# Keys and values of five batches made ahead, and three projections of the second attention in rounded parts

## Time and profile before

| | |
|---|---|
| median of 3 executions | 1377.33 us (1376.74 to 1379.98) |
| the profiled execution's own time | 1384.91 us |
| its span, first to last instruction | 1383.1 us |
| mean granted TensorE clock | 0.975 of 2.4 GHz |
| PE busy | 1311.7 us, 95% |
| DVE, ACT, POOL busy | 65%, 57%, 43% |
| attention(0), to about | 356 us |
| moe0, from about | 363 us to 804 us |
| attention(1), to about | 1191 us |

### The profile page before, as it was taken

One profiled execution on the slowest core, in us unless ns is written; L12 is line 12 of the kernel. 1 busy time (PEld: TensorE's weight loads), 2 busy tenths in 40 slices (PEclk: granted clock), 3 DMA queues, 4 the chain that ended last, 5 costly groups with the idle time before them and its releaser, 6 DMA issues.

```text
span 1383.1 us, 37361 instructions
## 1 busy us (share of the span) xinstructions
PE 1311.7 (95%) x14572; PEld 1155.6 (84%) x14572; DVE 901.4 (65%) x2468; ACT 793.5 (57%) x1750; POOL 596.3 (43%) x522
## 2 busy tenths in 40 slices
PE   6999999998799999999999979999999999899898
PEld 5888888886699999999999968888998998655476
DVE  4788888886576555555655026888888886412287
ACT  3666666564377777777776425556555665332354
POOL 1244444343287777877776033433333431100131
PEclk9999999999699999999999978999999999999999
DMA  5574545461467777777776711731111110399912
GB/s 194 196 246 147 175 144 179 142 224 50 170 209 229 229 226 220 222 222 223 225 224 223 308 54 33 240 136 47 48 48 48 48 40 17 134 415 430 370 56 70
DMA packets 103614, 237.19 MB, mean 171 GB/s; under 512 B 8976, under 2 KB 85904, under 8 KB 91024
## 3 DMA queue, kind: packets, MB, share of 16 engines
q1 hardware_dynamic: 97296, 218.02, 45.7%
q0 software_dynamic: 6144, 16.79, 4.0%
HBM read 173.96 MB, written 60.82 MB: 170 GB/s over the span
## 4 chain that ended last, share of the span: by engine, by line
PE 86%; DVE 6%; DMA 3%; issue 2%; ACT 2%; POOL 1%; SPq 0%; DVEq 0%; ACTq 0%; PEldq 0%; POOLq 0%
PE ps L1337 13%; PE psT L1322 7%; PE psS L520 5%; PE ps L686 5%; PE ps L641 5%; PE psT L529 4%; PE ps L546 4%; PE ps L653 4%; PE ps L552 4%; PE psS L1322 3%; PE ps L1322 3%; PE ps L577 3%; PE ps L626 2%; PE ps L660 2%; PE psT L535 2%
## 5 line engine op out<-in xcount | busy, mean ns | idle before, releaser
L1290 POOL TENSOR_TENSOR wb_lo<-arena,wb_hi 128x2048 fp32r<-128x2048 f32 x64 | 296.4, 4632 | 97.8 <-ACT wb_hi L1409 97.8
L1337 PE MATMUL ps<-wb_hi,hT_hi 128*128 128x256 f32 x528 | 152.4, 289 | 0.8 <-DVE hT_lo L1463 0.8
L529 PE MATMUL psT<-arena 32*128 32x128 f32 x2048 | 152.4, 287 | 0.0
L1006 POOL TENSOR_TENSOR arena<-arena,eps_sb 128x1 f32<-128x1 f32 x96 | 23.9, 249 | 291.7 <-DVE arena L878 198.9
L1337 PE MATMUL ps<-wb_lo,hT_hi 128*128 128x256 f32 x528 | 147.7, 280 | 0.0
L1337 PE MATMUL ps<-wb_hi,hT_lo 128*128 128x256 f32 x528 | 147.6, 280 | 0.0
L520 PE MATMUL psS<-arena 32*128 32x256 f32 x1024 | 143.3, 399 | 0.7 <-ACT arena L798 0.7
L1409 ACT CAST wb_hi<-arena 128x1024 fp32r<-128x1024 f32 x128 | 130.5, 1045 | 8.1 <-DMA arena<-w_dram 7.6
L529 PEld LDWEIGHTS psT<-arena 32*128 32x128 f32 x2048 | 127.7, 190 | 1.1 <-issue 1.1
L920 DVE TENSOR_REDUCE arena<-psS 128x8 f32<-128x1024 f32 x64 | 78.4, 1225 | 49.6 <-PE psS L520 49.6
L520 PEld LDWEIGHTS psS<-arena 32*128 32x128 f32 x1024 | 95.4, 192 | 13.4 <-issue 11.3
(11 more groups left out here) (325 smaller groups left out, 3704.8 us busy)
## 6 DMA issues: line engine op xcount, KB each, us to landing
arena<-wset_dram SPq DMA_DIRECT2D x24, 2048.0 KB, 14.5
xs_rows<-arena SPq DMA_DIRECT2D x33, 1024.0 KB, 8.3
arena<-w_dram SPq DMA_DIRECT2D x32, 1028.0 KB, 6.1
arena<-w_dram SPq DMA_DIRECT2D x32, 1024.0 KB, 5.9
arena<-w_dram SPq DMA_DIRECT2D x7, 2052.0 KB, 12.3
w_sb<-xs_rows SPq DMA_DIRECT2D x33, 256.0 KB, 2.7
xs_rows<-arena SPq DMA_DIRECT2D x33, 256.0 KB, 5.5
arena<-ctxT_dram SPq DMA_DIRECT2D x63, 128.0 KB, 2.3
```

The costliest lines, as they stand in the source:

```text
L529: nc.tensor.matmul(psT[:, b, j * P:(j + 1) * P], kbd[p, (k - 1) % 3, c, par, :], qT[p, (k - 1) % 3, c, :], start=j == 0, stop=False, skip_ ...
L1290: nc.gpsimd.tensor_tensor(wb_lo[:, u % 2, part], wb_raw[:, u % 2, part], wb_hi[:, u % 2, part], ALU.subtract).then_inc(w_g.sem, 1)
L1337: last = nc.tensor.matmul(ps[5][:, t * D:(t + 1) * D], hp[:, f, t * P:(t + 1) * P], wp[:, f, :], start=f == 0 and t == 0 and n == 0, stop= ...
```

## The change

**Five batches ahead.** Keys and values of batches 3 to 7 of attention(1) are made in the last steps of attention(0). SP issues five loads of ctx (128 KB each) at step B-1, into ctxT, xh and xT, after the last queries. PE makes keys 0 of the five in step B+2 after 577's place, its values after 609's place, the second batch after the product at 696, the third to fifth after 708. ACT copies each PSUM bank of 128x512 to SBUF (`put_away`), the first two in the steps, the others at the start of routing. PE waits for all five copies before `turned(0)`. In attention(1), the steps for these batches have no keys and values on PE; ACT reads kbd and vz from the stash. Their ctx loads of 128 KB leave attention(1).

**Rounded parts.** A helper `thrice` makes three float32r products in place of one f32 product. It is used for the values of the batches from 8 on (24 of them), the output projection of all 32 batches, and the dv projection of all 32. ACT makes the rounded weights (three copies of 128x512 after the early batches), POOL the rests (three subtractions in steps 0 to 2). For each batch from 8 on, POOL makes ctx_hi and ctx_lo (128x256 each) one step ahead; for each batch, POOL makes x1_hi and x1_lo (128x256 each) after 769; ACT writes aT in rounded form, and DVE makes aT_lo (128x256 from PSUM) ahead of the maxima at 920. Both POOL pairs stand ahead of 1046 in POOL's stream.

**Moves.** The slots' table is loaded at step B+2, after the last output projection, and no longer at step 9. In unit 0 of moe0 the first weight roundings for unit 1 stand after gelu 1 and gelu 2.

```diff
+                    if A and k == B - 1:
+                        sp.wait_ge(kv_p.sem, kv_p.at(B - 1, "V"))
+                        sp.wait_ge(pre_p.sem, pre_p.at(B - 1, "Q"))
+                        for n_ in range(STASH):
+                            sp.dma_start(stash_ctx[n_]..., a["ctxT"][3 + n_]).then_inc(ld_stash[n_], 16)
...
-                    if not A and k == 5 + EARLY_SETS:
+                    if not A and k == B + 2:
+                        sp.wait_ge(o_p.sem, o_p.at(B - 1, "O"))
                         sp.dma_start(dead[:, 0:12 * P], a["slots"]).then_inc(ld_slots, 16)
...
+                def thrice(out_, left, right):
+                    for n_, (i_, j_) in enumerate(((0, 0), (0, 1), (1, 0))):
+                        for c in range(C):
+                            last = nc.tensor.matmul(out_, left[i_][:, c, :], right[j_][:, c, :],
+                                                    start=n_ == 0 and c == 0, stop=n_ == 2 and c == C - 1)
...
                 def values(i, bank):
+                    if not A and i >= early:
+                        pe.wait_ge(ctx_g.sem, ctx_g.at(i, "lo"))
+                        return thrice(ps[bank][:, D:2 * D], (ctx_hi, ctx_lo), split["v1"]).then_inc(kv_p.sem, 1)
...
+                def ahead_keys(n):
+                    if n == 0:
+                        pe.wait_ge(ld_w, 16)
+                        pe.wait_ge(ex_a.sem, ex_a.at(B - 1, "b"))
+                    pe.wait_ge(ld_stash[n], 16)
+                    ...
...
-                    if valid(k + 1) and k + 1 >= early:
+                    if valid(k + 1) and k + 1 >= early and not stashed(k + 1):
...
+                            pe.wait_ge(aT_v.sem, aT_v.at(k - 2, "lo"))
+                            last = thrice(ps[7][:, D:2 * D], (aT_hi, aT_lo), split["o1"])
...
+                        pe.wait_ge(x1_g.sem, x1_g.at(k - 4, "lo"))
+                        thrice(ps[5][:, D:2 * D], (x1_hi, x1_lo), split["dv"]).then_inc(x1_p.sem, 1)
...
                         last.then_inc(prep_p, 1)
+                        ahead_keys(1)
+                        ahead_values(1)
...
+                        for n_ in range(2, STASH):
+                            ahead_keys(n_)
+                            ahead_values(n_)
...
+                def put_away(n):
+                    act.wait_ge(stash_p, n + 1)
+                    nc.scalar.copy(stash[n], ps[stash_bank[n]][:, :]).then_inc(stash_a, 1)
...
+                    if not A and valid(out_i):
+                        dve.wait_ge(av_a.sem, av_a.at(out_i, "aT"))
+                        before(dve, o_p.sem, o_p.at(out_i - 1, "O"))
+                        nc.vector.tensor_tensor(aT_lo[:, :, :], ps[7][:, 0:D]..., aT_hi[:, :, :], ALU.subtract)
...
+                    if not A and valid(k - 4):
+                        pool.wait_ge(x1_a.sem, x1_a.at(k - 4, "xT"))
+                        before(pool, x1_p.sem, x1_p.at(k - 5, "V"))
+                        nc.gpsimd.tensor_scalar(x1_hi[:, :, :], v, 1.0, 0.0, ALU.mult, ALU.add).then_inc(x1_g.sem, 1)
+                        pool.wait_ge(x1_g.sem, x1_g.at(k - 4, "hi"))
+                        nc.gpsimd.tensor_tensor(x1_lo[:, :, :], v, x1_hi[:, :, :], ALU.subtract).then_inc(x1_g.sem, 1)
+                    if not A and valid(k + 2) and k + 2 >= early + STASH:
+                        ...ctx_hi, ctx_lo in the same way, after the load of batch k+2
...
+                pe.wait_ge(stash_a, STASH)
                 turned(0)
...
-                    if u == 0:
-                        rounded_half(1, 0, 0)
-                        rounded_half(1, 0, 1)
+                        if u == 0 and b in (1, 2):
+                            rounded_half(1, 0, b - 1)
```

More of the change, by code:

```diff
@@ L29 @@
 EARLY_SETS = 4
+STASH = 5
 EARLY_PAIRS = 6
@@ L142, in build @@
         att = carve(H, DH)
+        aT_at = place[0]
         aT = carve(C, P)
@@ L151, in build @@
         mrest = carve(G, 4)
+        spare_at = place[0]
         xn = carve(3, D)
@@ L228, in build @@
         place[0] = max(place[0], attention_used)
+        stash_near = carve(4, 2 * D)
         yb = carve(2, 2, D)
         zero = carve(D)
-        xoff = carve(C, 2 * P)
-        assert place[0] <= attention_end, place[0]
+        assert stash_near is not None and place[0] <= attention_end, place[0]
         place[0] = max(attention_used, 12224)
@@ L451, in attention, with stashed, kv @@
             early_bank = (6, 7, 3)
+            if not A:
+                ctx_g = track(n + "ctx_g", "hi lo", B, base=-2 * (early + STASH))
+            def stashed(i):
+                return not A and early <= i < early + STASH
+            def kv(i):
+                return i if A or i < early else i - STASH
             def ctx_of(i):
@@ L728, in values, with stashed_keys, stashed_values @@
                         .then_inc(kv_a.sem, 1)
+                def stashed_keys(i):
+                    for par in range(2):
+                        last = nc.scalar.activation(kbd[:, i % 3, :, par, :],
+                                                    stash[i - early][:, 0:D].rearrange("p (c t) -> p c t", c=C), ACT.Identity,
+                                                    bias=0.0, scale=cv["parity"][:, par:par + 1])
+                    last.then_inc(kv_a.sem, 1)
+                def stashed_values(i):
+                    nc.scalar.copy(vz[:, i % 3, :, 0, :], stash[i - early][:, D:2 * D].rearrange("p (h d) -> p h d", h=H))\
+                        .then_inc(kv_a.sem, 1)
+                def put_away(n):
+                    act.wait_ge(stash_p, n + 1)
+                    nc.scalar.copy(stash[n], ps[stash_bank[n]][:, :]).then_inc(stash_a, 1)
                 if A:
@@ L741, in scalar @@
                         values(i, early_bank[i])
+                    for name in ("o1", "v1", "dv"):
+                        nc.scalar.copy(split[name][0][:, :, :], w[name]).then_inc(hi_a.sem, 1)
                 for k in steps:
@@ L1124, in scalar @@
             def scalar(act):
+                for n in range(2, STASH):
+                    act.wait_ge(stash_p, n + 1)
+                    nc.scalar.copy(stash[n], ps[stash_bank[n]][:, :]).then_inc(stash_a, 1)
                 act.wait_ge(route_v.sem, route_v.at(0, "ex"))
```

109 lines of the change are left out of this document (88 added, 21 removed).

## The result

The changed kernel takes 1368.95 us in the median of seven executions (1366.81 to 1373.01), the kernel before 1378.74 beside it (1376.74 to 1380.67). The ratio is 0.9933, 95% interval 0.9919 to 0.9947: 9.8 us faster where 17.6 were forecast. The time lies inside the range given, 1353 to 1372, and away from the forecast of 1359.7.

A forecast was written before the change was run, and what follows sets the result against it. PE was taken to bound attention(1), with engines and transfers taking turns at the border to moe0. Rounding 13.6, five batches 4.0 and border 0 sum to 17.6 us, from 1377.33 to 1359.7 us, range 1353 to 1372.

The forecast's parts named there:

- Rounding, 13.6 us: Attention(1), PE: 88 projections as six float32r products each save 0.155 us, 13.6 us in all.
- The upper bound of 28: Most the rounding could gain: 88 x 0.87 x 3/8, about 28 us, with each pass a quarter and loads free.
- aT_lo and POOL's work, cost 0: Attention(1) steps: DVE's added 0.42 us and POOL's added 2.9 us a step fit into slack, cost 0.
- 0.3 us of DVE's slack is left: Attention(1) step: after aT_lo's delay of 0.47 us, DVE keeps 0.3 us of slack at its tightest point.
- The rule against the change: Shared SBUF port: POOL's work beside 942 and 956 could stretch them, 0.45 us a step against 0.3 of slack.
- POOL late with x1_lo: Fifth rival, ahead of dv: POOL operations of 1.5 us make PE wait; 1385.8 us, slower; chance 0.05.
- Five batches, 4.0 us: Attention(1): five steps without keys and values gain 0.8 us each, the rest becoming waits for att; bounds 0 and 8.8.
- DVE stays behind PE by a hair: Attention(1), the five steps without keys and values: 892 ends at 961.43, then aT_lo, 920 at 961.9 instead of 962.0.
- The border, 0: Attention(0) to moe0: `turned(0)` 1.7 us later, offset by a shorter unit 0; net 0, ends -3.0 and +5.6.
- the fourth (the batches only move, 1366.1): Rival: the five steps wait for att, 4.0 us lost, and the border costs 2.4; 1366.1 us; chance 0.13.
- the first (the clock comes back at the border): Rival: the batches fill PE's gaps, so full clock returns and stays; border -3.0, 1356.7 us; chance 0.15.
- The second (DVE becomes the bound): Rival: aT_lo's 0.42 us and stretched operations find no slack; loop gives back 13.4, 1373.1 us; chance 0.13.

The follow-up runs named there:

- e7: Changed kernel with POOL's rounding of ctx moved behind the gathers and the weights' low parts to the top of k = 0 to 2; 1370.15 us.
- e2: Changed kernel without the rounding: five batches still made ahead, values, output and dv in float32; 1378.74 us, ratio 0.9988 to the kernel before.
- e1: Changed kernel without the five batches ahead, rounding kept; 1371.15 us, ratio 0.9949 to the kernel before.
- e11: e2 with the 17 small VectorE operations for single units moved ahead of the expert stage; 1374.71 us, ratio 0.9967.
- e15: Changed kernel with only the 17 small VectorE operations for single units moved ahead of the expert stage; 1366.64 us, ratio 0.9902.
- e4: Changed kernel with the output projection in float32 again, so no aT_lo; 1365.0 us, a single time without interval.
- e16: e13 with the low parts of v1 and dv made at the top of k = 2 and 3; 1363.27 us, ratio 0.9873.
- e6: Changed kernel with dv of the last three batches in float32 and dv's low part in another place; 1365.85 us, ratio 0.9917.
- e14: e1 with the 17 small operations moved ahead of the stage, ctx rounded behind the gathers, last three batches' dv in float32; 1366.44 us, ratio 0.9905.
- e13: Changed kernel with 17 small operations moved ahead of the stage, ctx rounded behind the gathers, last three batches' dv in float32; 1361.89 us, ratio 0.9890.
- e8: Changed kernel with batches 10 to 14 made ahead instead of 3 to 7; 1370.24 us.
- e10: Changed kernel without batches ahead, with POOL's new order and dv of the last three batches in float32; 1370.1 us, ratio 0.9929.
- e12: Kernel before with only the 17 small VectorE operations for single units moved ahead of the expert stage; 1379.03 us, ratio 1.0002.

## Why the prediction was right or wrong

**Where the 17.6 us went,** second trace against second, 8.9 us in all. In k = 7 to 31 lie 71 of the 88 rounded products: 11.0 forecast, 9.7 measured. In k = 2 to 7 lie the five lighter steps and ten rounded products: 5.6 forecast, 2.7 measured. In the tail lie six: 0.9 forecast, 1.4 lost. Start and border lost 1.3, k = 0 to 2 lost 2.2, and the stage behind unit 1 gained 1.4; differences of that size stand between two traces of one kernel too. So the step that failed for certain is the price of the other engines' chains where PE's own work shrinks: DVE's in the lighter steps was put too low, POOL's in the tail at nothing.

**Rounding, 13.6 us: right in mechanism and in the price of a product, too large in sum.** The steady period was forecast as 10.65 and is 10.66. But 71 products gave 9.7 us, not 71 x 0.155 = 11.0. Every fourth or fifth step is a long one, and e7, without the long ones, gives 10.4; the rest is the price, 0.15 a product. The ten products in k = 2 to 7 were to give 1.6 and gave nothing (49.8 us in the changed kernel, 49.7 in e2, where they are float32): DVE ends last there. In e1, with fourteen rounded products there, it was 0.4, and PE idled 1.3 us for DVE. In the tail it was a loss. By the timed medians the rounding is worth 7.7 to 9.8 us (before to e1, e11 to e15, e2 to the changed kernel). The upper bound of 28 does not follow from its own words: four instructions' time less three quarters of it leaves 88 x 0.87 / 4 = 19. Nothing was built on it.

**aT_lo and POOL's work, cost 0: wrong in two places, right in one.** POOL's plain copy was cheaper than assumed, 0.40 and not 0.73. aT_lo cost nothing in full steps that e4 could show, but in k = 2 to 7 e4 is 0.7 us shorter without it. In full steps the part that failed is "0.3 us of DVE's slack is left". The sum had no stretched operation in it. The rule against the change priced that of 942 and 956 alone, which kept their 412 ns in the median (the changed kernel's L1058 is 413, with five of 22 at 0.60 to 0.62, one ahead of each long step), and not the four small operations ahead of them, which grew by 0.5 to 1.2 us. (The working also starts 920 at 962.32, before aT_lo ends at 962.37; that slip of 0.05 us changes nothing.) The Trainium skill (SBUF — State Buffer, Who interferes with whom) says that GpSimd works through the port pair that is VectorE's second, that whoever issues first has it "for the whole instruction", and that a VectorE operation with two SBUF inputs contends for it with a GpSimd operation that reads SBUF, as casts can. The traces agree that the VectorE operation is held to the end of the GpSimd one, to 0.05 us; that the first to issue wins they don't show, since in e16 the VectorE operation started first, beside a gather, and was held to the end of the subtraction behind it. I had read the effect off the one line that shows it least.

**POOL late with x1_lo: no wait in full steps, right; in the tail, wrong.** The working tested dv in a full step only. Behind the last scores nothing covers POOL's 1.15 us; PE waited 1.9 and 0.3 there. e6's trace is 3 us shorter, of which 1.5 at full clock are shown to be this chain's.

**Five batches, 4.0 us: the term that failed most for its size.** The wait of 609 for att came about as forecast, 0.8 to 1.2 us in these steps. They gave 2.3 to 2.75 in k = 2 to 7 (1.5 between the repaired kernels, e14 to e13), and nothing that can be told in k = 0 to 2. e8 showed the reason in full steps: "DVE stays behind PE by a hair" is false, since with 0.8 us less on PE it is DVE's chain that ends last, at 10.4 us.

**The border, 0: near the truth as a sum for this change, but by luck, since errors offset each other.** The working's `turned(0)` at 364.4 leaves out the copy of 0.59 that it names: 359.0 + 5.3 + 0.59 is 364.9. In fourteen traces with the batches ahead, `turned(0)` came at 34.0 us on average behind the last step, in six without at 30.4: 3.6 later, where 1.7 was forecast for a full clock. Unit 1 came 19.5 us behind it before, 17.7 with POOL's halves started sooner (e1, e10, e14) and 16.5 with the batches too. So the halves alone are worth 1.8 us, with no part in what the change is named for, and the batches cost 3.6 - 1.2 = 2.4 net. That eats what they gain in the steps. These numbers scatter from one trace to the next (31.7 to 38.2 in the fourteen, 29.0 to 32.1 in the six), and of the fourteen those with the highest have the most time at 1.2 GHz at the border: 27 us in e7's, 24 in e15's and e16's, 10 in the changed kernel's first.

**And the double stall,** which no part of the working had: it is in two of the ten traces with the batches ahead and the small operations in their old place, in none of the four without batches, and costs 6 to 8 us. What the five batches are worth once it is removed, e13 against e14 gives as 4.5 us by medians, but 0.0015 in the ratios, whose intervals overlap; the stages say 2.4 lost at the border against 1.5 to 2.75 gained in the steps. Between nothing and 4 us, and these runs don't settle it further. The moved slots' table and the five loads, costed at nothing, left no mark: the tail is 217.26 us in e2 (no stretch at 1.2 GHz in it) and 218.9 in e11 (3.4 us of one, as in before's 218.5 to 218.9).

Of the rivals, the fourth (the batches only move, 1366.1) came nearest in time and in place; the first (the clock comes back at the border) was half right, since it did come back in most traces from the second batch on, and unit 1 came only 1.2 us sooner behind `turned(0)` with the batches. The second (DVE becomes the bound) was right for steps without keys and values, and for every fourth or fifth step otherwise.

## What to carry to other kernels

Before work goes to GpSimd, list VectorE's small operations with two SBUF inputs, and its casts, that will run beside it: each can wait for a whole GpSimd instruction, so they belong where GpSimd is idle, and long GpSimd instructions away from chains of them. Work taken off the bounding engine pays only down to the next engine's chain; measure that chain's own length, here 10.4 us in a step of 10.66. And cost an added link once in a full step and once in the drain, where nothing hides it.

## What was not expected of the hardware

A VectorE operation of eight elements or six took 4.46 to 4.62 us in sixteen instances, each beside a GpSimd subtraction of 128x2048 (4.5 to 4.7 us). In e12's edit the same operations took 0.17 to 0.22. Operations with one input from PSUM beside the same subtractions, such as hT_lo at 0.69 us, were not held. One trace's clock at start-up was worth 3.5 us: a stage table needs two traces of each kernel.
